# Attention rounds of a macaron block: input split in pairs, low parts of the output one round later, one value product inside the last round

## The reference

```python
x = x + 0.5 * ffn(layernorm(x))
x = x + attention(layernorm(x))
x = x + 0.5 * ffn(layernorm(x))
# attention(inputs):
x = conv1d(inputs, conv_w, taps=3, padding='SAME') + conv_b      # 1024 -> 3 * 256
q, k, v = split(x, 3)                                            # 256 wide, blocks of 128 tokens
qh, kh, vh = q @ wq + bq, k @ wk + bk, v @ wv + bv               # 16 heads of 64
scores = where(causal, (qh / 8) @ kh.T, -1e9)                    # within a block of 128
o = softmax(scores) @ vh
return (o @ wo + bo) @ proj_w + proj_b
```

## Time and profile before

| | |
|---|---|
| median of 3 runs | 1018.08 us (1016.97 to 1020.89) |
| profiled execution, its own time | 1019.92 us |
| its span | 1018.1 us |
| PE busy | 916.2 us, 90% of the span |
| DVE busy | 715.1 us, 70% |
| ACT busy | 419.6 us, 41% |
| POOL busy | 360.4 us, 35% |
| mean granted TensorE clock | 0.989 of 2.4 GHz |

### The profile page before, as it was taken

How to read it: one execution, slowest core, us unless ns; L and a number is a source line. 1 busy time by engine, 2 the same in 40 slices (tenths; PEclk the granted TensorE clock), 3 DMA queues, 4 the chain that set the end, 5 groups by cost and what they waited for, 6 DMA issues and landing times.

```text
span 1018.1 us, 15266 instructions
## 1 busy us (share of the span) xinstructions
PE 916.2 (90%) x4992; PEld 697.7 (69%) x4992; DVE 715.1 (70%) x1491; ACT 419.6 (41%) x1127; POOL 360.4 (35%) x305
## 2 busy tenths in 40 slices
PE   4788989898899999999988998998899798999997
PEld 2466667675433677788766786777677576887885
DVE  5677777679998898655586488189458857667552
ACT  3533333221134326243675356256435544433331
POOL 2144444546653221000233133133133432554565
PEclk9999999999999999999999999999999999999999
DMA  9432332333224341684003032212153485333432
GB/s 289 157 125 88 122 117 89 116 112 105 92 94 132 131 146 68 227 290 173 14 11 93 2 83 85 62 41 72 52 136 84 143 256 159 125 125 146 133 115 104
DMA packets 43012, 119.97 MB, mean 118 GB/s; under 512 B 7232, under 2 KB 16448, under 8 KB 41536
## 3 DMA queue, kind: packets, MB, share of 16 engines
q1 hardware_dynamic: 42944, 119.11, 35.8%
HBM read 87.64 MB, written 31.46 MB: 117 GB/s over the span
## 4 chain that ended last, share of the span: by engine, by line
PE 61%; DVE 21%; issue 7%; ACT 6%; DMA 3%; POOL 2%; SPq 0%; POOLq 0%; DVEq 0%; ACTq 0%
PE a_p_g L1846 17%; PE a_p_g L634 11%; PE f_p_m L634 6%; PE c_p_m L1292 4%; PE c_p_m L1294 3%; PE c_p_m L1296 3%; PE c_p_m L1295 3%; PE a_p_s L1870 2%; PE a_p_o L1894 2%; ACT a_s L1642 2%; DVE a_sums L1746 2%; PE a_p_s L577 1%; DVE f_nst L399 1%; DVE a_s L1743 1%; DVE a_pt L1760 1%
## 5 line engine op out<-in xcount | busy, mean ns | idle before, releaser
L1575 POOL TENSOR_TENSOR a_s<-a_s,a_sums 128x512 f32<-128x512 f32 x64 | 66.6, 1040 | 279.6 <-DVE a_sums L1752 279.6
L280 POOL TENSOR_TENSOR f_y<-f_y,f_res 128x512 f32<-128x512 f32 x64 | 84.3, 1317 | 143.7 <-DVE f_y L492 143.0
L1642 ACT ACTIVATE a_s<-a_s,a_nmx 128x128 f32<-128x128 f32 x256 | 99.3, 390 | 41.1 <-DVE a_nmx L1748 41.1
L634 PE MATMUL f_p_m<-f_wsign,f_a_hi 128*128 128x512 f32 x256 | 106.4, 416 | 0.0
L1846 PE MATMUL a_p_g<-c_xs_hi,x_room 128*128 128x512 f32 x256 | 94.6, 417 | 10.1 <-DVE c_xs_lo L1708 9.5
L634 PE MATMUL f_p_m<-f_wsign,f_a_lo 128*128 128x512 f32 x256 | 102.5, 400 | 0.0
L634 PE MATMUL a_p_g<-f_wsign,f_a_hi 128*128 128x512 f32 x256 | 102.5, 400 | 0.0
L634 PE MATMUL a_p_g<-f_wsign,f_a_lo 128*128 128x512 f32 x256 | 100.4, 392 | 0.0
L277 POOL TENSOR_TENSOR f_res<-f_res,f_hbias 128x512 f32<-128x512 f32 x64 | 84.2, 1316 | 8.7 <-DMA f_res<-x_after_attention 6.2
L1292 PE MATMUL c_p_m<-c_vf,c_ring_f 128*128 128x512 f32 (+1 forms) x192 | 73.9, 542 | 7.0 <-DVE c_ring_f L964 6.9
L1294 PE MATMUL c_p_m<-c_vh,c_ring 128*128 128x512 f32 x192 | 75.4, 393 | 5.2 <-issue 2.9
(11 more groups left out here) (222 smaller groups left out, 2200.8 us busy)
## 6 DMA issues: line engine op xcount, KB each, us to landing
c_raw<-in_conv_w_dram SPq DMA_DIRECT2D x24, 768.0 KB, 4.3
f_w_raw<-in_w_t_dram SPq DMA_DIRECT2D x8, 1024.0 KB, 11.0
f_res<-in_x_dram SPq DMA_DIRECT2D x16, 512.0 KB, 4.3
x_after_ffn<-f_y SPq DMA_DIRECT2D x8, 1024.0 KB, 6.4
f_xin<-x_after_attention SPq DMA_DIRECT2D x8, 1024.0 KB, 5.0
f_res<-x_after_attention SPq DMA_DIRECT2D x16, 512.0 KB, 4.3
out_dram<-f_y SPq DMA_DIRECT2D x8, 1024.0 KB, 6.3
f_xin<-in_x_dram SPq DMA_DIRECT2D x7, 1024.0 KB, 5.0
```

The lines of the kernel that those rows point to most:

```text
L280: pool.tensor_tensor(y[:, p, t, h], y[:, p, t, h], res[:, t, h], ALU.add).then_inc(y_done, 1)
L634: last = pe.matmul(p_m[:, q % 2, :], part[p][:, k, q // 2 * P:q // 2 * P + P], wsign[:, k, q % 2 * HALF:q % 2 * HALF + HALF], start=(k == ...
L1575: pool.tensor_tensor(s[:, r], s[:, r], sums[:, r].unsqueeze(2).broadcast_to([P, 4, P]), ALU.mult).then_inc(probs_ready, 1)
L1642: done = act.activation(s[:, r, h, :], s[:, r, h, :], ACT.Exp, bias=nmx[:, r, h:h + 1], scale=SCALE, accum_out=sums[:, r, h:h + 1])
```

## The change

```diff
     if not last:
         for n, part in enumerate((0, 2, 1, 3)):
             rounds[14 + n].append(("qk", 1, part))
-        after = [("v", 1, n) for n in range(2 * GT)] + after
+        rounds[ROUNDS - 1].append(("v", 1, 0))
+        after = [("v", 1, n) for n in range(1, 2 * GT)] + after
     return rounds, after
 
 TAKES_FIRST = (0, 2, 4, 6, 8, 10, 14, 15)
-SPLIT_ROUNDS = (11, 12, 13, 14, 15, 16)
+LOW_ROUNDS = (8, 12, 16, 19)
+SPLIT_ROUNDS = (11, 11, 13, 13, 15, 16)
 
@@ vector, body
-                    if u >= V_LAG + 3 and (u - V_LAG - 3) % 4 == 0:
-                        quad = (u - V_LAG - 3) // 4
+                    if u in LOW_ROUNDS:
+                        quad = LOW_ROUNDS.index(u)
                         for i in range(2):
                             c = 2 * quad + i
                             dve.wait_ge(o_hi, KH * g + c + 1)
```

## The result

Median 1015.81 us over 20 runs (1012.91 to 1021.01), against 1019.68 us for the kernel before over 20 runs. The ratio is 0.9962, with a 95% interval of 0.9945 to 0.9979: 3.9 us won, where 7.0 was forecast. The forecast of 1011.1 started from the median of three runs, 1018.08; against the 1019.68 of twenty it lies 8.6 lower. The profiled execution took 1014.58 us, its span is 1012.8 us.

What follows compares the result with a forecast made beforehand. The chain of waits was 61% PE, 21% DVE, so the gaps of PE that DVE leaves counted. Groups 0, 1, 2 and last gave 1.9 + 2.3 + 2.3 + 0.5 = 7.0 us, 1018.08 becoming 1011.1 us; range 1006 to 1017.

Steps and rivals of the forecast that it cites:

- Low parts in round 12, wait at round 13: Low parts queued behind both splits in round 12; P·V of round 13 waits for them, 0.45 us later.
- First and third product of the next group: Rounds 14 and 16 on PE: splits ready earlier, so these products start 1.4 and 3.35 us earlier.
- The failed step: Round 17, group 1: DVE, through the exponentials, limits P·V to 633.45 instead of 634.60, keeping 1.15 of 3.35 us.
- the last P·V: Round 19, group 1: products after it begin 0.93 us earlier, plus 1.39 for one product fewer, 2.3 us won.
- its term of 1.9: Group 0: 0.5 us at the last P·V plus 1.39 for the value product; between 0.5 and 3.5.
- my signs of being wrong: P·V waits of 1.3 us at rounds 9 and 17, low clock in rounds 13 to 15, or ACT awaiting a chunk.
- (b): New half-clock stretches after the wait before P·V of round 13, groups 1 and 2; 3.0 us lost, 1014.1 us; chance 0.12.
- Last group: Only low parts move; reciprocal and copy fit the DVE's wait for ACT in round 15; 0.5 us won (0 to 1.5).
- Value product: One value product moved into PE's wait in round 19, behind split 5; worth between 0.65 and 1.39 us a group.
- (a): DVE paces rounds 12 to 18, only the value product pays: 1.9 us won, 1016.2 us; chance 0.18.
- (d): Low parts directly before P·V of rounds 9, 13, 17 cost PE 1.32 us at 12 places: 1019.4 us; chance 0.07.

Runs made afterwards that it cites:

- fill: Changed kernel plus matmuls nobody reads in PE's waits before P·V of rounds 13 and 17, groups 0 to 2; 1013.46 us, 0.9946 of the kernel before.
- low_first: Changed kernel with the DVE's low parts moved ahead of the low splits and the last group's row statistics; 1015.31 us, 0.9951 of the kernel before.
- no_value: Changed kernel without the value product in round 19; 0.9994 of the kernel before, 3.2 us above the changed kernel.
- value_only: Kernel before with only one value product moved into round 19; 0.9988 of the kernel before.
- low_only: Kernel before with only the low parts moved one round later; 1.0020 of the kernel before.

## Why the prediction was right in sign and wrong in size

**Low parts in round 12, wait at round 13.** Forecast: 0.45 later than before against group 1's clock, measured 0.65 (616.83 against 619.89, with the groups' clocks 3.7 apart by the scores of round 12). Right in kind and nearly in size.

**First and third product of the next group.** Forecast 1.4 and 3.35 earlier; measured in group 2 1.3 and 3.1. Right.

**The failed step** is round 17, in both its parts. The first is the start time. I wrote that P·V "starts at 633.45 instead of 634.60", 1.15 us earlier; measured it is 0.7 in group 1 and 0.8 in group 2. On group 1's clock (3.70 added) it started at 633.93: the DVE had the exponentials at 630.32 instead of 630.1, the reciprocal, which I named and gave no time, took 0.2, and P·V started 0.15 behind the low parts where I took 0.05. This passes on to the last P·V: 0.93 forecast, 0.47 measured in group 2. It is why groups 1 and 2 win 1.8 us each at full clock and not 2.3. In group 0 the same step is wrong by more: 0.75 earlier was forecast, 0.0 measured (56.01 against 56.04), and the last P·V came 0.3 later where 0.5 earlier was forecast, with one stretch of 3.5 us at half clock in either profile. So its term of 1.9 came at 1.0, and at 1.6 in the second pair, where the kernel before had the longer half clock. What of the DVE's work made group 0 worse than the others I have not taken apart.

The second part is the wait. By my own times PE is free more than 2 us ahead of its P·V: from 627.3 come the third and fourth product and two steps of transposes, to about 631.0. I never wrote that gap down, though a wait of 1.3 us at round 17 stood among my signs of being wrong. The wait of 2.5 us was new, and half clock follows it in one middle group of each profile of the changed kernel, 1.2 us each time. I had put the half clock into rival (b), at the wait of round 13, with 0.12. fill shows that waits 13 and 17 together carry it: with PE kept busy in them, groups 0, 1 and 2 take 1.2, 1.1 and 0.0 us less.

How much of the miss that is: by the two pairs of profiles 4.4 us are won of 7.0. Of the missing 2.6, about 1.1 is groups 1 and 2 at full clock, 0.6 group 0, 0.3 the last group, and 0.6 that the changed kernel's two profiles hold one half-clock stretch more in groups 1 and 2 than the two before. The last is not shown to be a difference of the kernels: the mean granted clock is 0.979 over the 20 executions of the changed kernel, and 0.978 to 0.979 over the 66 of the kernel before that were timed beside the experiments. The size of the DVE's path to round 17 is the shown part; the clock is not.

**Last group.** Forecast +0.5; measured -0.5 in the first pair of profiles and +0.8 in the second. So its sign stays open. In the first pair P·V of round 15 came 0.96 later (59.16 us after the first scores instead of 58.20), with new waits of 0.71 at round 9 and 0.36 at round 13 ahead of it; round 17 won 0.47 of it back, as forecast. The wait at round 9 was forecast as 0.2 to 0.6, but I left it out of the sum. It isn't what carries the loss: in low_first it is gone and P·V of round 15 still comes at 59.03.

**Value product.** Forecast between 0.65 and 1.39. Measured 0.45 alone, and by the estimate from no_value 0.47 in the changed kernel: below the range, because the product waits about 0.78 us for the split before it starts (value_only) and P·V stands behind it.

**Rivals.** (a), only the value product pays, is refuted: at full clock a middle group wins 1.8 us, of which the value product is 0.5. (b), new half-clock stretches, came at round 17 instead of round 13, but the kernel before has them too, so as an explanation of the miss it isn't shown. (d), low parts directly ahead of P·V, was given 0.07. Its wait exists at round 17 (1.28 us in low_only, 2.5 in the changed kernel), at round 13 it replaced a wait for the copy that was nearly as long, and at round 9 of groups 1 and 2 there is none. Even for the low-part edit alone its sum doesn't hold, as the last P·V is not later. I did not see that the edits don't add; I summed them in order and never asked what ACT's second high split does to the DVE's 0.90 us if the low parts stay. In the changed kernel the DVE has no wait ahead of its low parts in round 12 (the row at 615.29): the pairs delay ACT's high parts at just the point from which the low parts were taken.

## What to carry to other kernels

When a wait is removed, follow the engine to its next wait and write down that wait's length, not only the time at which it ends: a gap that merely moves still costs if the clock falls behind it. Give every instruction on the way a time; 0.2 us left out at two places made a fifth of a group's forecast wrong. A good place for a piece of work is where two engines already stand for a third; here moving 1.3 us of DVE work from behind the exponentials into the idle ahead of them was worth more than three edits that removed visible waits. Time edits of one schedule singly and together before summing them. And compare groups at the same clock: in low_only and no_value, lengths and starts read across a half-clock stretch pointed to sizes that full clock doesn't show.

## What the hardware showed that I had not expected

A fall of the granted clock isn't a fixed property of a place: the same code with the same waits (1.76 and 2.45 us) had it in group 1 in one execution and in group 2 in another, and the kernel before had it behind waits of 1.13 and 1.65 us once and not another time. In group 0, behind the same wait of 3.44 or 3.45 us, the half clock lasted 3.5 us in one execution of the kernel before and 6.9 in the other, with another 3.5 a little later. In the middle groups one such stretch cost 1.2 to 1.3 us of a group's 86 to 88.
